# An attention layer and a routed feed-forward on one core: the front half rewritten, with norms in the weights, routing inside the attention, and rows sent to a region of each expert

## The reference

```python
# attention: 16 query heads in 4 groups, 4 key heads, head width 16
qh = rope(layernorm(x) @ Wq); kh = rope(ctx @ Wk); vh = ctx @ Wv
scores = einsum('bghsd,bhad->bhsa', qh, kh)        # summed over the 4 groups g
out = (softmax(scores / 4) @ vh).mean(over the 4 key heads) @ Wo
x = x + tanh(g_xattn) * out
# feed-forward: 8 experts of inner width 1024, the best 2 for each token
h = layernorm(x); probs = softmax(h @ gate_w.T); w, idx = top_k(probs, 2); w = w / w.sum()
y = sum over the two experts of w * (silu(g) * u @ down.T),  with g, u = split(h @ gate_up.T)
x = x + tanh(g_ffn) * y
```

## Time and profile before

| what | value |
| --- | --- |
| median of 3 runs (lowest, highest) | 495.59 us (495.37, 497.58) |
| span of the profiled execution | 495.3 us |
| busy: PE, PEld, DVE, ACT, POOL | 90%, 72%, 47%, 40%, 50% |
| mean granted clock of TensorE | 0.936 |
| end of the first key projection (L594) | 12.65 us |
| transfers of 256 KB on SP's queue, issue to landing | 2.2 to 2.4 us |
| the page's chain: experts' matmuls L765 and L785, issue | 18%, 10%, 17% |

### The profile page before, as it was taken

How to read it: one execution, slowest core, us unless ns; L and a number is a source line. 1 busy time by engine, 2 the same in 40 slices (tenths; PEclk the granted TensorE clock), 3 DMA queues, 4 the chain that set the end, 5 groups by cost and what they waited for, 6 DMA issues and landing times.

```text
span 495.3 us, 10419 instructions
## 1 busy us (share of the span) xinstructions
PE 443.8 (90%) x2456; PEld 355.6 (72%) x2457; DVE 233.8 (47%) x481; ACT 198.6 (40%) x458; POOL 249.2 (50%) x222
## 2 busy tenths in 40 slices
PE   4986888997589999999999999999999999999960
PEld 2654555554247888888888788888888888888850
DVE  2789998667972433333342433334243324424320
ACT  1364555444024332562462462346234624623320
POOL 1336555205462232486487397239734863972421
PEclk9997777887579999999999999999999999999996
DMA  8901333211341111245136135213621461112220
GB/s 291 368 23 43 126 114 112 75 65 42 99 173 33 23 24 32 32 129 169 32 106 199 30 112 188 35 32 106 193 37 26 119 189 32 22 22 32 37 34 11
DMA packets 20327, 44.16 MB, mean 89 GB/s; under 512 B 4256, under 2 KB 15536, under 8 KB 17232
## 3 DMA queue, kind: packets, MB, share of 16 engines
q1 hardware_dynamic: 13632, 34.44, 20.2%
q0 software_dynamic: 6672, 9.46, 11.0%
HBM read 34.91 MB, written 8.98 MB: 89 GB/s over the span
## 4 chain that ended last, share of the span: by engine, by line
PE 45%; issue 17%; DMA 10%; DVE 10%; POOL 9%; POOLq 3%; ACT 2%; DVEq 1%; ACTq 1%; SPq 0%
PE bank L765 18%; PE bank L785 10%; DMA out<-x,idx_s 5%; DMA small<-xn_scratch,idx_g 4%; POOL dn L291 4%; PE bank L775 3%; PE bank L647 2%; PE bank L711 2%; PE bank L633 2%; POOL gu L291 2%; PE bank L663 2%; DVE probs L946 1%; DVE xn L934 1%; POOL xT L339 1%; DVE negmax L957 1%
## 5 line engine op out<-in xcount | busy, mean ns | idle before, releaser
L765 PE MATMUL bank<-gu,xT 128*128 x816 | 201.1, 395 | 0.8 <-ACT xT L522 0.8
L765 PEld LDWEIGHTS bank<-gu,xT 128*128 128x128 f32 x816 | 148.5, 188 | 29.3 <-issue 1.3
L1105 DVE TENSOR_TENSOR x<-x,bank 128x512 f32<-128x512 f32 x68 | 46.8, 688 | 170.3 <-ACT x L529 170.2
L785 PE MATMUL bank<-dn,hT 128*128 x816 | 113.9, 289 | 4.6 <-DVE x L1122 4.0
L785 PEld LDWEIGHTS bank<-dn,hT 128*128 128x128 f32 x816 | 101.3, 189 | 6.0 <-issue 6.0
L529 ACT ACTIVATE x<-bank 128x512 f32<-128x512 f32 x68 | 40.6, 597 | 109.5 <-PE bank L765 105.3
L291 POOL TENSOR_TENSOR gu<-wraw,gu 128x2048 f32 (+1 forms) x16 | 77.1, 4817 | 4.8 <-ACT gu L430 4.7
L357 POOL DMA_INDIRECT out<-x,idx_s x34 | 54.7, 1610 | 28.8 <-POOL idx_s L354 28.8
L347 POOL DMA_INDIRECT small<-xn_scratch,idx_g x37 | 37.6, 1017 | 30.6 <-POOL idx_g L344 30.6
L1109 DVE TENSOR_TENSOR hT<-bank,hT 128x512 fp32r<-128x512 f32 x68 | 46.5, 684 | 3.2 <-ACT hT L533 3.2
L344 POOL COPY idx_g<-idx 128x1 int32 (+1 forms) x37 | 11.3, 305 | 68.0 <-DMA out<-x,idx_s 44.5
(11 more groups left out here) (131 smaller groups left out, 447.4 us busy)
## 6 DMA issues: line engine op xcount, KB each, us to landing
wraw<-in_gu SPq DMA_DIRECT2D x16, 1024.0 KB, 5.0
wraw<-in_dn SPq DMA_DIRECT2D x8, 1024.0 KB, 4.9
x<-in_x SPq DMA_DIRECT2D x8, 256.0 KB, 7.7
out<-x SPq DMA_DIRECT2D x8, 256.0 KB, 2.4
xn_scratch<-xn SPq DMA_DIRECT2D x8, 256.0 KB, 2.2
area<-in_ctxT SPq DMA_DIRECT2D x2, 480.0 KB, 6.5
small<-xn_scratch,idx_g POOLq DMA_INDIRECT x37
out<-x,idx_s POOLq DMA_INDIRECT x34, 3.9
```

The costliest lines, as they stand in the source:

```text
L765: mm = nc.tensor.matmul(bank[2 * hf + n][:, :], xT[:, par, xp, k, :], gu_part(where, wp, k * 2 * I + col, HALF), start=(k == 0 and xp == 0 ...
L785: mm = nc.tensor.matmul(bank[6][:, 0:D], hT[:, hf, hp, j * P:(j + 1) * P], dn_part(where, wp, (hf * JH + j) * D, D), start=(hf == 0 and j ...
L1105: V.tensor_tensor(h[:, hf, :], silu[:, hf, :], bank[2 * hf + 1][:, :], ALU.mult).then_inc(h_made, 1)
```

## The change

The expert loop's products stay as they are; nearly all that is ahead of them is new.

- **First norm.** x comes from the host in transposed form too. Wq is centred once (its column mean, found by a product with ones, is taken off), so that x itself can be projected; the reciprocal deviation goes into the scale and bias of the exponentials, one for each row. `normalise`, its transposes and their copies go.
- **Softmax.** The values carry a column of ones, and the product of values gives the denominators; results of 17 columns a head are divided, not the probabilities. For that the product is turned around: eight matmuls a batch with 17 columns each, then a transposition of the result. Four heads' outputs are projected with Wo stacked four times.
- **Routing.** The centred router weights act on x and on the attention's output in the same PSUM bank, so the logits come with the output projection. Two maxima, compares and ranks are done in five sets of batches within the attention's loop; the second norm's factor is carried in the row.
- **Rows.** Each expert has a region in a scratch of DRAM. POOL scatters each tile twice, once for each choice (32 indirect transfers of 128 rows). The one-hot products go. In the expert loop, ACT loads each block's 128 rows with one plain transfer, two steps ahead, and norms them as it stages them.
- **Splits.** Only expert 0's pieces are split ahead, by POOL in four chunks each, in rounds 0 to 2; expert 1's are split in the loop, as its scratch holds keys and probabilities before.
- **Loads.** ACT's queue carries five of the first loads.

The order of the attention's loop is new on each engine (below); nothing of it is in flight two rounds apart any more but the scores. The diff, cut:

```diff
+SETS = ((0, 1), (2, 3), (4, 5), (6,), (7,))
...
-            for q in range(3):
-                load_piece(q)
-            sp.wait_ge(zrow_ready, 1)
+            load_piece(0)
+            load_piece(1)
+            load_xT(sp, 2)
+            load_x(sp, 4)
+            load_piece(2)
+            load_x(sp, 5)
+            load_xT(sp, 3)
+            load_x(sp, 6)
+            load_x(sp, 7)
...
-                sp.wait_ge(xn2_ready, TB * (b + 1))
-                sp.dma_start(xn2_v[:, TB * b:TB * b + TB, :], xn2[:, :, :]).then_inc(xn2_out, 16)
...
+            sp.wait_ge(ends_ready, 1)
+            for e in range(E):
+                end = sp.value_load(ends_i[0:1, e:e + 1], min_val=0, max_val=REGION - P)
+                sp.dma_start(rows_d[bass.ds(end, P), :], x_d[T:T + P, :]).then_inc(fill_rest if e else fill_first, 16)
             for q in range(6, 3 * E):
                 load_piece(q)
...
+            def split_low_first(p):
+                pool.wait_ge(w_hi, p + 1)
+                for n in range(PIECE // CHUNK):
+                    nc.gpsimd.tensor_tensor(chunk_of(1, p, n), wraw[:, p * PIECE + n * CHUNK:p * PIECE + (n + 1) * CHUNK],
+                                            chunk_of(0, p, n), ALU.subtract).then_inc(w_lo_first, 1)
...
+                nc.gpsimd.tensor_scalar(tmp, var[:, TB * b:TB * b + TB, 1], EPS, scale, ALU.add, ALU.mult)\
+                  .then_inc(pool_step, 1)
...
+            def power(var, b, scale, out, sig):
...
+                nc.gpsimd.tensor_tensor(out, tmp, expo[:, 0:1].broadcast_to([P, TB]), ALU.pow).then_inc(sig, 1)
+            def score_scale(b):
+                pool.wait_ge(moments1, TB * (b + 1))
+                power(mv, b, float(HD), rs[:, TB * b:TB * b + TB], rs_ready)
+            def second_norm(b):
+                pool.wait_ge(moments2, TB * (b + 1))
+                rstd = x[:, TB * b:TB * b + TB, D + RSTD]
+                power(mv2, b, 1.0, rstd, rstd2_ready)
+                pool.wait_ge(rstd2_ready, 2 * b + 1)
+                tmp = mean_rstd[:, b % 2, :]
+                n_step[0] += 1
+                nc.gpsimd.tensor_tensor(tmp, mv2[:, TB * b:TB * b + TB, 0], rstd, ALU.mult).then_inc(pool_step, 1)
+                pool.wait_ge(pool_step, n_step[0])
+                nc.gpsimd.tensor_scalar(x[:, TB * b:TB * b + TB, D + SHIFT], tmp, -1.0, None, ALU.mult)\
+                  .then_inc(rstd2_ready, 1)
...
+            def send_rows(b):
...
+                for t in range(TB * b, TB * b + TB):
+                    for k in range(2):
+                        nc.gpsimd.indirect_dma_start(
+                            out=rows_d, out_offset=bass.IndirectOffsetOnAxis(ap=slot[:, t, k:k + 1], axis=0),
+                            in_=x[:, t, :], in_offset=None).then_inc(scattered, 16)
...
+            for t in range(B):
+                second_norm(t)
                 if t + 2 < B:
-                    spread_keys(t + 2)
-                if 1 <= t <= 4:
-                    split_low(*divmod(t - 1, 3))
-            split_low(1, 1)
...
+                    score_scale(t + 2)
+                if t <= 2:
+                    split_low_first(t)
+                for b in range(B):
+                    last = SETS[SET_OF[b]][-1]
+                    if last + 1 + (b != last) * 0 + (len(SETS[SET_OF[b]]) == 2 and b == last) == t:
+                        send_rows(b)
+            pool.wait_ge(w_lo_first, 3 * (PIECE // CHUNK))
+            pool.sem_inc(w_lo, 3)
+            for b in range(B):
+                last = SETS[SET_OF[b]][-1]
+                if last + 1 + (len(SETS[SET_OF[b]]) == 2 and b == last) >= B:
+                    send_rows(b)
...
+            def exponentials(b, j):
...
+                for hh in range(KVH):
+                    ins = nc.scalar.activation(probs[:, j, hh, :], score_ps(j)[:, hh, :], ACT.Exp,
+                                               bias=shift[:, j, hh:hh + 1], scale=rs[:, t:t + 1])
+                ins.then_inc(exp_done, 1)
...
+                copy_pT(t, 0)
+                copy_pT(t, 1)
...
+                nc.scalar.activation(oT[:, :], oT_ps, ACT.Copy).then_inc(oT_ready, 1)
+                if t + 1 < B:
+                    exponentials(t + 1, 1)
...
-            for t in range(NT):
-                nc.scalar.activation(marked[:, :, t, :], oh[:, :, t, :], ACT.Copy,
-                                     scale=const[:, t0 + t:t0 + t + 1]).then_inc(marked_ready, 1)
...
+                elif t <= 3:
+                    split_high(0, t - 1)
...
+            def load_rows(s, q):
+                base = act.value_load(tab[0:1, 4, bass.ds(s, 1)], min_val=0, max_val=REGION - P)
+                act.dma_start(xg[:, q, :], rows_d[bass.ds(base, P), :]).then_inc(x_loaded[q], 16)
...
+            def stage(s, q):
+                act.wait_ge(x_loaded[q], 16 * ((s >> 1) + 1))
+                nc.scalar.activation(xs[:, :], xg[:, q, 0:D], ACT.Identity, scale=xg[:, q, D + RSTD:D + RSTD + 1],
+                                     bias=xg[:, q, D + SHIFT:D + SHIFT + 1]).then_inc(x_staged, 1)
...
+            def attend(b):
...
+                if b - 1 in ENDS:
+                    ranks(ENDS[b - 1])
+                for j in range(TB):
+                    at = TB * b + j
+                    nc.tensor.matmul(att[:, j, 0:D + E], oT[:, P * j:P * (j + 1)], wo[:, :], start=True, stop=False)
+                    for k in range(KC):
+                        mm = nc.tensor.matmul(att[:, j, D:D + E], xT_all[:, k, P * at:P * (at + 1)], gc[:, k, :],
+                                              start=False, stop=(k == KC - 1))
+                mm.then_inc(att_psum, 1)
...
+            def ranks(g):
...
+                nc.tensor.matmul(out, ones_bf[:, :], base_bf[:, :, :].broadcast_to([P, wide, E]), start=True, stop=False)
+                for t in range(a):
+                    nc.tensor.matmul(out, ones_bf[:, :], chosen[:, t:t + 1, :].broadcast_to([P, wide, E]),
+                                     start=False, stop=False)
...
+            for t in range(B):
+                transpose_probs(t, 0)
+                if t + 1 < B:
+                    scores(t + 1, 0)
+                transpose_probs(t, 1)
+                if t + 1 < B:
+                    scores(t + 1, 1)
+                mix_values(t)
+                if t % 2 == 0 and t // 2 + 1 < 4:
+                    project_q(t // 2 + 1)
+                transpose_o(t)
+                attend(t)
+            ranks(NS - 1)
...
-            for m in range(2 * NT):
-                t, k = m // 2, m % 2
-                pe.wait_ge(marked_ready, t + 1)
-                nc.tensor.matmul(bank[1][0:NCOL, 0:P], marked[:, k, t, :], row, start=(m == 0),
-                                 stop=(m == 2 * NT - 1)).then_inc(onehot_used, 1)
-            pe.wait_ge(slotT_ready, 1)
-            nc.tensor.transpose(bank[2][:, 0:NCOL], slotT, ident[0:NCOL, 0:NCOL]).then_inc(slots_psum, 1)
...
-            stay_warm(5)
-            pe.wait_ge(idx_ready, 1)
+            pe.wait_ge(pT_copied, TB * B)
+            stay_warm(10)
...
+            def softmax_shift(b, j):
...
+                link(V.tensor_reduce(negmax[:, j, :], score_ps(j), AX.X, ALU.max, negate=True))
+                if j == 0:
+                    dve.wait_ge(rs_ready, b + 1)
+                V.tensor_scalar(shift[:, j, :], negmax[:, j, :], rs[:, t:t + 1], None, ALU.mult).then_inc(shift_ready, 1)
...
+            def normalise_o(b):
...
+                link(V.reciprocal(rden[:, :, :], o_ps[:, :, :, HD]))
+                V.tensor_tensor(on[:, :, :, :], o_ps[:, :, :, 0:HD],
+                                rden[:, :, :].rearrange("p j (h o) -> p j h o", o=1).broadcast_to([P, TB, KVH, HD]),
+                                ALU.mult).then_inc(on_ready, 1)
...
+            def best_two(b):
...
+                for j in range(TB):
+                    V.max(top[:, TB * b + j, :], att[:, j, D:D + E]).then_inc(dve_step, 1)
...
+                V.tensor_tensor(ties[:, TB * b:TB * (b + 1), :, :],
+                                att[:, :, D:D + E].rearrange("p j (k e) -> p j k e", k=1).broadcast_to([P, TB, 2, E]),
+                                top[:, TB * b:TB * (b + 1), 0:2].rearrange("p j (k e) -> p j k e", e=1)
+                                .broadcast_to([P, TB, 2, E]), ALU.is_equal).then_inc(top_done, 1)
...
+            def choose(g):
...
+                link(V.tensor_tensor(both, both, c("prio").rearrange("p (o q e) -> p o q e", o=1, q=1)
+                                     .broadcast_to([P, n, 2, E]), ALU.mult))
...
+                first_of(0)
+                link(V.scalar_tensor_tensor(out=ties[:, a:z, 1, :], in0=pick[:, a:z, 0, :], scalar=-2.0 * E,
+                                            in1=ties[:, a:z, 1, :], op0=ALU.mult, op1=ALU.add))
+                first_of(1)
+                V.tensor_tensor(chosen[:, a:z, :], pick[:, a:z, 0, :], pick[:, a:z, 1, :], ALU.add)\
+                 .then_inc(chosen_ready, 1)
...
```

(38 more changed lines are left out.)

1027 lines of the change are left out of this document (473 added, 554 removed).

## The result

The changed kernel takes 514.3 us (median of 4 runs, 513.28 to 514.59) against 495.5 for the one before on the same chip: a ratio of 1.036, 95% interval 1.034 to 1.039. The forecast was 487.7 in a range of 469 to 506, and faster. The sign is wrong and the time is outside the range. The rival with this sign, a starved TensorE clock, gave 504.

A forecast was written before the change was run, and what follows sets the result against it. TensorE was seen busy for 94% of the expert loop and 84% of the attention. The forecast summed 121.5 us to the last output projection, 27.3 to the experts, 338.6 of loop and 0.3 around: 487.7, range 469 to 506.

The forecast's parts named there:

- a starved TensorE clock: Slower rival, attention: the tight loop lowers TensorE's clock, below about 0.75 TensorE sets the period; +11 us, 504 in all; chance 0.27.
- The expert loop: Loop start to end: steps stay 9.45 us, gather stalls of 5.3 us go, expert 1's splits cost nothing; 338.6 us.
- The low clock at its start: TensorE, idle before the experts, then runs 5 us at half speed: 2.5 us added.
- Before the attention: Kernel start to first output projection: terms in series behind the key projection end at 36 us, 3.6 later than before.
- The period of the attention: Between output projections: DVE's 5.5 us, then 3.1 of transposes, copy and projection; 8.6 a period, 57.5 for seven.
- set 3's choice and gap: Routing on DVE inside the attention: a choice at 1.7 us and a gap at 0.4.
- the ranks' 3.1: Ranks on TensorE ahead of the attention's output projection: 5 to 16 matmuls, 3.1 us in all.
- What waits on POOL: Attention: DVE waits for score scales behind second norms; 4.7 us in periods without a split, 9.5 in three with one.
- From attention to experts: Last output projection to experts: DVE, second norm, twelve scatters at 1.02, landing, load and staging; 24.75 us, fills hidden.
- The scatters are held up: Rival between attention and experts: DVE's table instructions delay twelve scatters by 0.5 us each; 494 in all; chance 0.07.

## Why the prediction was wrong

*The expert loop*: right. From the third transposition on they are 9.45 us apart, but for one of 9.76 near the end that the kernel before has too, and the splits of expert 1 inside it cost nothing. The low clock at its start was sized too small: from the first product to the third transposition it takes 14.65 us instead of 10.90, 3.75 more and not 2.5. *Before the attention*: right in its end, 35.8 for 36; its terms were not checked one by one.

*The period of the attention* (8.6 us; 57.5 for seven): this step failed. It was a sum at TensorE's full clock. The output projection and its router products, 2.0 us in the sum, take 2.43 at 2.4 GHz and 4.32 at 1.2 GHz. All seven in the periods ran low: 29.8 us, where 17.0 would be seven at the full clock (an estimate, 7 x 2.43) and 14.0 were in the sum. DVE waits for each of them. The products ahead of them fell less: the transposition of the outputs takes 0.63 or 0.64 instead of 0.41 in three periods of seven, and the product of values 3.59 instead of 1.96 in the last only. Ahead of that transposition TensorE waits for DVE, 0.6 to 5.9 us in a period, and behind it 0.5 for ACT's copy. The last period, which has no shifts and a single wait for POOL, of 1.1 us, shows it nearly bare: 12.63 at a clock of 0.50, where the sum had 5.9, 2.1 for set 3's choice and gap, and some of the ranks' 3.1. Kernels with POOL's order mended put a second size on it: periods 85.0 at 0.70 and 74.7 at 0.95. This was named as the slower rival, "below about 0.75 granted in the attention TensorE and not DVE sets the period", priced at 11 us; the clock came out at 0.64. The page of the Trainium skill that the prediction named for this rival (TensorE: Matmul & The Clock Gate, "HAM oscillation — how this bites in real kernels") agrees with these rows, and the argument set against it, that long stretches of small matmuls ran at the full clock, weighed too much: in the kernel before such a stretch (50.06 to 55.60 us, with eight products of 8 columns in 1.06) has no pause in it, while the transpositions behind its pause of 1.42 us took 1.96 and not 1.04.

*What waits on POOL* (4.7 and 9.5, in all 14.2): the size was right, the waits on POOL come to 13.9 (12.8 and 1.1), and mending the order gave 10.3 us back in one execution and 8.6 by the medians. So the 14.2 us by which the periods missed, a like number by chance, lie outside of these waits. The split into periods was off: the fourth, charged with split and scatters at 3.15 us, has a single wait of 4.29 and choices held for 2.4, since POOL's split waits for ACT's rounded part of the next round (5.93 us), a wait that the prediction did not see in POOL's order.

*From attention to experts* (24.75): failed where it said that DVE's tables "and the eight fills on SP lie beside the scatters". The tables do. The fills stand in SP's list behind a load that waits for POOL's release of the buffer, and that release stands behind POOL's whole attention loop. The change moved neither line in a way that looks costly: the wait in `load_piece` and the `sem_inc` in POOL's list had to be read together. The release gave 4.9 us, ACT's order and its share of the fills 2.0; 27.9 remain, 3.1 more than the 24.75 (the 2.5 for the clock belong to the loop). The scatters, taken at 1.02 us, come 1.27 apart: 12 of them, 3.0 us more, which by its size is that rest.

```profile
L390 POOL DMA_INDIRECT rows_scratch<-x,slot x12 | 11.8, 985 | 3.8 <-issue 3.5 <-DVE x L1029 0.3
```

Busy time alone (985 ns) is nearly the row's 0.98 that the price was taken from the earlier trace rows; the 0.30 of idle time between two was not in it. "The scatters are held up" did not come true: under DVE's tables (to 152 us) and after them they take 0.96 us alike, but for the first, 1.07, and one of 1.16. The rule of the Trainium skill (SBUF — State Buffer, the "DVE blocks DMA" trap) is for a DVE instruction in a mode that uses both ports. Whether one of these small table instructions runs in it no run shows, so the rows don't test the rule; they show that its price of 0.5 us a scatter did not come.

Two errors of one sign, then: 14.2 us in the periods and 10.0 in the tail. Of the tail's, 6.9 are SP's and ACT's lists and 3.0 the spacing of the scatters. In the periods the output projections alone are 15.8 over their term, 12.8 of it the clock and 3.0 a full-clock price of 2.43 taken at 2.0; that is more than the whole, so other terms came out smaller, and which ones was not taken apart. The slower rival had cause and sign right; its 504 charged POOL 6 us more, which did not come, and lacks the 10 of the tail.

## What to carry to other kernels

When a change makes a pipelined stretch into a tight loop, work out its period twice, with TensorE at each of its two clocks, and take the slow one unless something keeps TensorE busy through the waits. For each wait that a change adds or keeps, ask where in the other engine's list the release stands, and what else stands behind the waiting instruction: here a release behind a loop and not inside it cost 5 us through three engines. Unused products for the clock are worth trying late and in several executions: six a round gave nothing in the changed kernel, four gave nothing with one period still held by POOL, and with its order mended four gave 3 us and seven up to 10, in the best of six executions.
